# Low halves of gelu moved to VectorE, and the steps around them reordered, in a two-layer graph network kernel

## The chip, the cores and the metric

One core of one Trainium2 chip runs the whole program. The metric is the device time of one launch in microseconds. The engines are TensorE (PE in the rows; PEld is its weight load), VectorE (DVE), ScalarE (ACT), GpSimd (POOL) and SyncE (SP, which issues the DMAs). Each takes its own instructions in the order written and waits on semaphores.

## The reference

```python
# 8 graphs, 1024 nodes, 256 features
h = maximum(layernorm(x), 0)                 # "new-graph norm"
for l in range(3):                           # layers 0 to 2
    si = h @ attn_w[l, :d]; sj = h @ attn_w[l, d:]
    s = leaky(si[:, :, None] + sj[:, None, :] + attn_b[l], 0.2)
    s = where(adj + eye > 0, s, -inf)
    h = layernorm(h + softmax(s) @ h, g1, beta1)
    h = layernorm(h + gelu(h @ W1 + b1) @ W2 + b2, g2, beta2)
x = x + h
h = maximum(layernorm(x), 0)                 # "graph norm" of the last layer
Wh = h @ W                                   # attention products
e = where(adj == 0, -1e9, leaky(Wh @ a1 [:, None] + Wh @ a2 [None, :], 0.2))
x = x + elu(softmax(e) @ Wh)
```

A row of the last layer without any edge gets the plain mean of Wh, for which the kernel needs the sum of Wh over all nodes of a graph.

## The kernel before, in words

The work is 32 steps, `ORDER`, k = 0 to 31; each is one layer of one graph. 24 are feed-forward steps (layers 0 to 2) and 8 are last-layer steps (6, 10, 14, 18, 22, 29, 30, 31). The order on each engine is written out by hand: each engine's block walks the steps with its own `ffn_step` or `gat_step`, and tables such as `MAX_FE`, `UNITS_FE`, `SHIFT_FE` say at which place t (0 to 7, the tiles of the aggregation) or 8 + n (n = 0 to 15, the feed-forward blocks) a piece of the next step's preparation is done. `prep_tables(k)` picks the tables by the kind of step k + 1.

A feed-forward step. TensorE aggregates tile t (`aggregate`, 16 products of pw and xx), VectorE adds the residual and takes its statistics (`residual1`), GpSimd makes the reciprocal deviation (`ln_rstd`), ScalarE normalises (`normalise_pair`), TensorE transposes (`transpose_h`). Then, for block n, `hidden(k, n)` writes one of two PSUM banks FB[n % 2], ScalarE applies gelu and makes the fp16 high half (`gelu`), and the low half, gelu minus its high half, is made by VectorE for even n and by GpSimd for odd n (`g_low` on each). `second(k, n)` multiplies both halves by W2. TensorE's order in block n is: preparation, graph attention pieces, `hidden(k, n + 2)`, `second(k, n)`. Blocks 0 and 1 of hidden stand inside the aggregation of tile 7. For even n + 2, `hidden` waits for VectorE's low half of block n, as it is made from the bank itself. For odd n + 2 it waits only for gelu, since odd gelus are written to a buffer g32 in SBUF, which GpSimd reads.

Preparation of the next step: VectorE's row maxima (`row_max`, tiles 0 to 7, with `shift_columns` after tiles 3 and 7), ScalarE's mask shifts (`shifted_mask`, tiles 0 to 7, at the places of a SHIFT table), then 16 units (`unit` on TensorE, `score` on VectorE, one place later) and `exps` on ScalarE. `scores(q, t)` on VectorE are the two dot products of a tile for step q.

Some steps carry more. RAW_AT: the first norm of a new graph (`raw_statistics`, `ln_rstd(LNR, ...)`, `normalise_pair(LNR, ...)`, `edges`, `self_edges`). GAT_AT: the graph norm and products of a last layer. There ScalarE copies a transposed pair (`gat_pair`), VectorE makes its low half (`gat_low`, tile mj), TensorE multiplies (`gat_product`, bank TH) and ScalarE writes the values (`gat_values`); `gat_colsum` sums them over nodes on TensorE as 8 fp32 products with ones in bank TP, and `gat_sum` copies the sum to csum on VectorE. g = 0 is carried by k=5 in its own order (GAT_FFN_LATE), g = 1 to 6 by k=8, 12, 16, 20, 24, 28, and g = 7 by the last-layer step k=29.

Of the kernel before, what the change touches and what calls it, by code (L numbers as in the profile page):

```python
# [86 lines left out]
GAT_FFN_LATE = {5}  # L87

# [36 lines left out]
SHIFT_FE = {7: (0,), 8: (1,), 9: (2,), 10: (3,), 12: (4, 5), 13: (6, 7)}  # L125
# [3 lines left out]
SHIFT_FC = {7: (0,), 8: (1,), 9: (2,), 10: (3,), 11: (4,), 12: (5,), 13: (6,), 14: (7,)}  # L129
# [4 lines left out]
def prep_tables(k):  # L134
# [9 lines left out]
    if q == 8:  # L144
        return dict(col=None, ct=1, s1=3, sj=5, r2=4, row=MAX_F8, units=UNITS_FE, shift=SHIFT_FE)
# [52 lines left out]
def build(nc, x, adj, attn_w, attn_b, W1, b1, W2, b2, g1, beta1, g2, beta2, gatW, gata, out):  # L198
# [10 lines left out]
    with ctx:  # L209
# [18 lines left out]
        g32 = sb("g32", [P, HALF])  # L228
# [64 lines left out]
        def xgT_of(g):  # L293
            return xgT7 if g == 7 else xgT
# [58 lines left out]
        cs_done = sem("cs_done")  # L353
        wct_done = sem("wct_done")
# [243 lines left out]
        def _(pool):  # L598
# [62 lines left out]
            def g_low(k, n):  # L661
                i = NF * fi(k) + n
                pool.wait_ge(ghi_done, i + 1)
                pool.tensor_tensor(out=gT[:, i % GRING, 1, :], in0=g32[:, :], in1=gT[:, i % GRING, 0, :],  # L664
                                   op=ALU.subtract).then_inc(glo_odd, 1)

# [21 lines left out]
            def ffn_step(k):  # L688
# [17 lines left out]
                else:  # L706
# [8 lines left out]
                    g_low(k, 1)  # L715
                    ln_rstd(LN1, i, 3)
                early = k + 1 not in VERY_LATE
                for n in range(NF):
                    if n % 2 == 1 and not (n == 1 and low_first):
                        g_low(k, n)  # L720
                    if n == 11:
                        ln_rstd(LN2, i, 0)
                    if n in (1, 3, 9, 11):
                        j = (1, 3, 9, 11).index(n)
                        affine(LN1, k, 2 * j)
                        affine(LN1, k, 2 * j + 1)
# [8 lines left out]
                    if raw is not None and early:  # L735
                        if n in (1, 3, 5, 7):
                            ln_rstd(LNR, raw, n // 2)
# [78 lines left out]
        def _(act):  # L816
# [30 lines left out]
            def gelu(k, n):  # L847
# [1072 lines left out]
```

## Time and profile before

| | us |
|---|---|
| median of 3 runs | 2521.38 |
| lowest and highest | 2520.96, 2524.68 |
| the profiled execution | 2526.61 |
| its span, first to last instruction | 2524.9 |
| busy: PE, DVE, ACT, POOL | 2296.6, 1834.2, 1581.8, 1278.9 |
| longest feed-forward steps: k=0, k=24, k=28 | 108.5, 100.7, 99.3 |

The busy times of the engines overlap. A wait row names the engine that stood idle, what it then did, and whose work ended last before it. Times inside the trace are counted from the span's start; step k=9 starts at 820.9 us, k=11 at 939.4, k=12 at 1028.8 and k=26 at 2120.7.

### The profile page before, as it was taken

To read this page: it belongs to the slowest core of one execution; us is meant where nothing else is said; L and a number is where in the kernel's file an instruction comes from. 1 tells how busy PE (TensorE), PEld (TensorE's weight loads), DVE (VectorE), ACT (ScalarE), POOL (GpSimd) and SP (SyncE) were. 2 spreads that over 40 slices of the span, in tenths; PEclk is the share of its full clock that TensorE was granted. 3 is DMA by queue.
4 is the path that set the end of the run, shared out by engine and by line. 5 is a ranking of instruction groups with operands and counts; after the bars stand their busy time and mean duration, and the time that the engine had idled before them with its cause. 6 is when DMAs were issued, how large, how long until landed. Compare 5 with 4: busy or idle time off the path is not lost.

```text
span 2524.9 us, 41684 instructions
## 1 busy us (share of the span) xinstructions
PE 2296.6 (91%) x14721; PEld 1736.3 (69%) x14721; DVE 1834.2 (73%) x4915; ACT 1581.8 (63%) x2426; POOL 1278.9 (51%) x2199
## 2 busy tenths in 40 slices
PE   5899999998899989999998999899998999999977
PEld 4566767766676766767766767677676677676766
DVE  8676678558677786776876878768777676766775
ACT  5467565757566675675766566765756656766654
POOL 4455456653365444663465552745535455545611
PEclk9999999998999999999999999999999999999998
DMA  6312021102210122110211101201131010101000
GB/s 217 109 43 88 9 81 50 57 4 67 76 59 5 38 72 71 59 39 6 92 55 55 43 25 68 87 24 43 40 103 60 1 43 10 38 5 26 22 22 26
DMA packets 66222, 128.57 MB, mean 51 GB/s; under 512 B 12985, under 2 KB 53213, under 8 KB 62942
## 3 DMA queue, kind: packets, MB, share of 16 engines
q1 hardware_dynamic: 66014, 125.90, 14.9%
q8 instruction: 117, 1.92, 0.3%
q14 instruction: 91, 0.75, 0.1%
HBM read 111.20 MB, written 14.68 MB: 50 GB/s over the span
## 4 chain that ended last, share of the span: by engine, by line
PE 52%; DVE 22%; POOL 9%; ACT 8%; issue 8%; DMA 1%; DVEq 0%; SPq 0%; POOLq 0%; ACTq 0%
PE OB L1609 35%; PE FBB L1609 10%; DVE mj L1216 4%; DVE pw L1240 4%; PE RB L1609 3%; DVE junk L1158 2%; ACT nms L888 2%; POOL xc L651 2%; POOL gT L664 2%; PE TH L1609 2%; DVE st L1107 2%; ACT gT L865 2%; POOL rs L633 1%; POOL xc L653 1%; DVE gT L1254 1%
## 5 line engine op out<-in xcount | busy, mean ns | idle before, releaser
L1609 PE MATMUL OB<-xx,pw 128*128 128x257 f32 x4096 | 958.3, 389 | 25.3 <-DVE xc L1134 11.3
L1609 PEld LDWEIGHTS OB<-xx,pw 128*128 128x128 f32 x4096 | 773.5, 193 | 160.4 <-DVE xc L1134 17.4
L1609 PE MATMUL FBB<-hT,wb 128*128 128x512 f16 x2304 | 564.2, 383 | 48.6 <-DVE gT L1254 37.9
L1609 PE MATMUL OB<-wb,gT 128*128 128x256 f16 x4608 | 575.1, 276 | 22.1 <-POOL gT L664 22.1
L1609 PEld LDWEIGHTS OB<-wb,gT 128*128 128x128 f16 x4608 | 453.3, 99 | 159.3 <-POOL gT L664 32.0
L664 POOL TENSOR_TENSOR gT<-g,gT 128x512 f16<-128x512 f32 x192 | 228.3, 1189 | 534.6 <-ACT gT L865 533.5
L1609 PEld LDWEIGHTS FBB<-hT,wb 128*128 128x128 f16 x2304 | 214.6, 98 | 255.0 <-DVE gT L1254 40.7
L871 ACT ACTIVATE pw<-pw,sj 128x512 f32<-128x512 f32 x512 | 336.6, 712 | 65.3 <-DVE pw L1240 64.3
L829 ACT ACTIVATE xc<-xc,nb,rs 128x256 f32<-128x256 f32 x384 | 212.8, 590 | 165.0 <-POOL nb L636 165.0
L651 POOL TENSOR_TENSOR xc<-xc,gb 128x256 f32<-128x256 f32 x384 | 294.0, 766 | 11.4 <-ACT xc L829 11.4
L888 ACT ACTIVATE nms<-nm,cc 128x1024 bf16<-128x1024 bf16 x256 | 281.3, 1136 | 18.7 <-DVE cc L1231 18.7
L1240 DVE SCALAR_TENSOR_TENSOR pw<-r2s,sj,RB 128x512 f32<-128x512 f32 x377 | 268.8, 739 | 32.3 <-PE RB L1609 31.9
L1254 DVE TENSOR_TENSOR gT<-FBB,gT 128x512 f16<-128x512 f32 x192 | 132.0, 687 | 219.8 <-ACT gT L865 218.6
L1216 DVE CUSTOM_DVE_ANT_0 mj<-RB,nm 128x1024 bf16<-128x1024 f32 x224 | 266.1, 1215 | 12.6 <-PE RB L1609 12.6
L628 POOL TENSOR_SCALAR ve<-mv 128x2 f32<-128x2 f32 x256 | 59.2, 231 | 399.9 <-DVE mv L1110 386.8
L860 ACT ACTIVATE FBB<-FBB,wc 128x512 f32<-128x512 f32 x192 | 126.3, 658 | 162.8 <-PE FBB L1609 162.1
L633 POOL TENSOR_TENSOR rs<-ve,mhalf 128x2 f32<-128x2 f32 x256 | 182.9, 715 | 21.3
L860 ACT ACTIVATE g<-FBB,wc 128x512 f32<-128x512 f32 x192 | 130.5, 680 | 100.5 <-PE FBB L1609 100.0
L1609 PE MATMUL RB<-identb,nms 128*128 128x128 bf16 x1508 | 137.4, 225 | 45.4 <-DVE pw L1240 35.9
L1117 DVE RECIPROCAL rden<-OB 128x1 f32<-128x1 f32 x192 | 31.9, 166 | 198.8 <-PE OB L1609 198.4
L1163 DVE CUSTOM_DVE_ANT_0 junk<-xx,aw 128x256 bf16<-128x256 f32 x256 | 163.2, 637 | 0.0
L1107 DVE BATCH_NORM_STATS2 st<-xc 128x6 f32<-128x256 f32 x392 | 156.7, 421 | 6.8
(127 smaller groups left out, 2721.8 us busy)
## 6 DMA issues: line engine op xcount, KB each, us to landing
wb<-w_scratch SPq DMA_DIRECT2D x19, 2048.0 KB, 7.9
adjst<-in_adj SPq DMA_DIRECT2D x56, 512.0 KB, 4.2
xx<-in_x SPq DMA_DIRECT2D x16, 512.0 KB, 5.5
nm<-in_L_gnn_W SPq DMA_DIRECT2D x6, 1024.0 KB, 8.4
gb<-in_L_gnn_g SPq DMA_DIRECT2D x48, 128.0 KB, 2.8
adjst<-in_x SPq DMA_DIRECT2D x6, 1024.0 KB, 10.9
out_x<-adjst SPq DMA_DIRECT2D x48, 128.0 KB, 1.7
pw<-in_adj SPq DMA_DIRECT2D x4, 1024.0 KB, 10.3
```

What stands on the lines that cost most here:

```text
L633: pool.tensor_tensor(out=rs[:, kind, c], in0=ve[:, kind, c], in1=mhalf[:, :], op=ALU.pow)\
L651: pool.tensor_tensor(out=v, in0=v, in1=gb[:, 0, :], op=ALU.mult).then_inc(mul_done[kind], 1)
L664: pool.tensor_tensor(out=gT[:, i % GRING, 1, :], in0=g32[:, :], in1=gT[:, i % GRING, 0, :], op=ALU.subtract).then_inc(glo_odd, 1)
L829: act.activation(dst, src, ACT.Relu if kind in (LNR, LNG) else ACT.Identity, bias=nb[:, kind, t:t + 1], scale=rs[:, kind, t:t + 1])\
L860: act.activation(dst, src, ACT.Gelu, bias=b1c[:, layer(k), f:f + 1], scale=1.0 / W_SCALE)\
L871: act.activation(v, v, ACT.Exp, bias=sj2[:, q % 2, jt:jt + 1]).then_inc(exp_done, 1)
L888: act.activation(nms[:, it, :], nm[:, slot(q), it, :], ACT.Identity, bias=cc[:, it:it + 1])\
L1107: dve.bn_stats(st[:, kind, t % 2, :], src[:, t, 0:D]).then_inc(bs_done[kind], 1)
L1163: dve.tensor_tensor_reduce(out=junk[:, 1, :], in0=src, in1=aw[:, l, 1, :], scale=1.0, scalar=0.0, op0=ALU.mult, op1=ALU.add, accum_out=sc[ ...
L1216: dve.tensor_tensor_reduce(out=mj[:, n % 2, :], in0=row_bank(q)[:, :], in1=nm[:, g % 3, t, :], scale=1.0, scalar=-3e38, op0=ALU.add, op1=A ...
L1240: dve.scalar_tensor_tensor(out=pw[:, jt, half], in0=r2s[:, half], scalar=sj8[:, q % 2, jt:jt + 1], in1=b, op0=ALU.max, op1=ALU.add).then_i ...
L1609: return pe.matmul(o, lhsT, rhs, start=first, stop=last)
```

## The change

- The low half of odd blocks is made by VectorE from the PSUM bank, like the even ones. The buffer g32 and GpSimd's `g_low` go. `hidden(k, n + 2)` now waits for the low half of block n for every n.
- New-graph norms: ScalarE's `normalise_pair(LNR)` moves from n = 2, 4, 6, 8 to n = 5, 7, 8, 9; GpSimd's `ln_rstd(LNR)` goes ahead of the affines of its block.
- `gat_product` stands one block later (n = 6, 8, 10, 12), `gat_values` too (7, 9, 11, 13), and the transposed pairs alternate between two buffers.
- Node sums of graphs 0 to 6: GpSimd adds the eight tiles (`node_sum`, 7 additions), TensorE does one product with ones, mostly in the step after.
- Mask shifts: SHIFT_FE and SHIFT_FC have tiles 0 to 3 at t = 6 and 7, ahead of the first gelu, and tiles 4 to 7 one a block; k=7 keeps the old table as SHIFT_F8.
- Scores of tiles 0 to 3 for steps 11, 15, 19, 23 move from the step three before them to n = 1, 3, 5, 7 of the step two before. `ln_rstd(LN2, i, 1)` and the second LN2 pair come one block earlier.

```diff
+SUM_AT = {k if k in GAT_FFN_LATE else k + 1: g for k, g in GAT_AT.items() if g < 7}
-SHIFT_FE = {7: (0,), 8: (1,), 9: (2,), 10: (3,), 12: (4, 5), 13: (6, 7)}
+SHIFT_FE = {6: (0, 1), 7: (2, 3), 11: (4,), 12: (5,), 13: (6,), 14: (7,)}
+SHIFT_F8 = {7: (0,), 8: (1,), 9: (2,), 10: (3,), 12: (4, 5), 13: (6, 7)}
-SHIFT_FC = {7: (0,), 8: (1,), 9: (2,), 10: (3,), 11: (4,), 12: (5,), 13: (6,), 14: (7,)}
+SHIFT_FC = {6: (0, 1), 7: (2, 3), 10: (4,), 11: (5,), 12: (6,), 13: (7,)}
...
+        xgT_odd = sb("xgT_odd", [P, 2, KD, 2 * P], f16)
...
-            return xgT7 if g == 7 else xgT
+            return xgT7 if g == 7 else xgT_odd if j % 2 else xgT
...
@@ gpsimd ffn_step
-                    if n % 2 == 1 and not (n == 1 and low_first):
-                        g_low(k, n)
+                    if raw is not None and early and n in (1, 3, 5, 7):
+                        ln_rstd(LNR, raw, n // 2)
+                    if n == (9 if k in GAT_FFN_LATE else 5) and k in SUM_AT:
+                        node_sum(SUM_AT[k])
...
+                if gat == 6:
+                    node_sum(gat)
...
+            def node_sum(g):
+                acc = csum[:, g % 2, :]
+                v = xx[:, g % 3, :, 0:D]
+                for t in range(1, NT):
...
+                    pool.tensor_tensor(out=acc, in0=v[:, 0, :] if t == 1 else acc, in1=v[:, t, :],
+                                       op=ALU.add).then_inc(part_done, 1)
@@ scalar
-                if n % 2 == 1:
-                    if i >= 2:
-                        act.wait_ge(glo_odd, i // 2)
-                    dst = g32[:, :]
-                else:
-                    dst = src
...
-                    if raw is not None and early and n in (2, 4, 6, 8):
-                        normalise_pair(LNR, raw, n // 2 - 1)
+                    if raw is not None and early and n in (5, 7, 8, 9):
+                        normalise_pair(LNR, raw, (5, 7, 8, 9).index(n))
-                        if n in (6, 8, 10, 12):
-                            gat_values(gat, n // 2 - 3)
+                        if n in (7, 9, 11, 13):
+                            gat_values(gat, (n - 7) // 2)
-                    if n == 15:
+                    if n == 14:
                         normalise_pair(LN2, k, 1)
@@ vector ffn_step
-                    if n % 2 == 0 and n > 0:
+                    if n > 0:
                         g_low(k, n)
+                    if n == 14 and k in SUM_AT and k not in GAT_FFN_LATE:
+                        gat_sum(SUM_AT[k])
+                    if k + 2 in AHEAD and n in (1, 3, 5, 7):
+                        scores(k + 2, n // 2)
@@ tensor
                 if i >= 2:
-                    if i % 2 == 0:
-                        pe.wait_ge(glo_even, i // 2)
-                    else:
-                        pe.wait_ge(gelu_done, i - 1)
+                    pe.wait_ge(glo_odd if i % 2 else glo_even, i // 2)
...
-                    if early and n in (5, 7, 9, 11):
-                        gat_product(gat, (n - 5) // 2)
+                    if early and n in (6, 8, 10, 12):
+                        gat_product(gat, (n - 6) // 2)
...
-                    if gat is not None and n == 14:
-                        gat_colsum(gat)
+                    if k in SUM_AT and n == (14 if k in GAT_FFN_LATE else 13):
+                        gat_colsum(SUM_AT[k])
```

## Rows read from the trace of the kernel before

**Rows 1.** the page's part 1: busy us, share of the span, instructions

```profile
PE 2296.6 (91%) x14721; PEld 1736.3 (69%) x14721; DVE 1834.2 (73%) x4915; ACT 1581.8 (63%) x2426; POOL 1278.9 (51%) x2199
```

**Rows 2.** by stretch (k=11, 12, 9): PE, PEld, DVE, ACT, POOL busy, clock, DMA

```profile
939.40:1028.80 89.40, 79.94 (x533) 59.37 (x530) 66.81 (x169) 54.09 (x83) 47.63 (x81) 0.99 0.21 68
1028.80:1124.40 95.60, 89.56 (x595) 68.08 (x594) 70.16 (x184) 60.95 (x97) 54.38 (x97) 0.99 0.13 40
820.90:904.90 84.00, 79.56 (x531) 59.05 (x531) 59.83 (x163) 51.26 (x78) 42.55 (x72) 1.00 0.10 34
```

**Rows 3.** waits of PE: us in total, times, longest us

```profile
PE FBB L1609 <- DVE gT L1254: 37.9, 32, 3.1
...
PE OB L1609 <- POOL gT L664: 22.1, 23, 2.6
PE TH L1609 <- DVE mj L1291: 19.1, 13, 2.6
```

**Rows 4.** groups by form: shapes, count, busy us, mean ns, idle before

```profile
L1240 DVE SCALAR_TENSOR_TENSOR pw<-r2s,sj,RB 128x512 f32<-128x512 f32 x377 | 268.8, 739 | 32.3 <-PE RB L1609 31.9
L1216 DVE CUSTOM_DVE_ANT_0 mj<-RB,nm 128x1024 bf16<-128x1024 f32 x224 | 266.1, 1215 | 12.6 <-PE RB L1609 12.6
L664 POOL TENSOR_TENSOR gT<-g,gT 128x512 f16<-128x512 f32 x192 | 228.3, 1189 | 534.6 <-ACT gT L865 533.5
...
L1163 DVE CUSTOM_DVE_ANT_0 junk<-xx,aw 128x256 bf16<-128x256 f32 x256 | 163.2, 637 | 0.0
...
L1254 DVE TENSOR_TENSOR gT<-FBB,gT 128x512 f16<-128x512 f32 x192 | 132.0, 687 | 219.8 <-ACT gT L865 218.6
...
L1609 PE MATMUL TP<-xx,onesf 128*128 128x256 f32 x128 | 29.3, 381 | 0.0
```

**Rows 5.** timeline of k=12, first blocks: start us, duration us, instruction, [idle before]

```profile
1056.95 1.13 ACT L888 ACTIVATE nms<-nm,cc 128x1024 bf16<-128x1024 bf16 x1
...
1058.10 1.28 ACT L860 ACT_TABLE_LOAD   x1
...
1059.86 0.66 ACT L860 ACTIVATE FBB<-FBB,wc 128x512 f32<-128x512 f32 x1 [0.48 <-PE FBB L1609]
...
1061.19 0.69 DVE L1254 TENSOR_TENSOR gT<-FBB,gT 128x512 f16<-128x512 f32 x1 [0.38 <-ACT gT L865]
...
1063.13 1.46 PE L1609 MATMUL FBB<-hT,wb 128*128 128x512 f16 x6
...
1069.94 1.47 PE L1609 MATMUL FBB<-hT,wb 128*128 128x512 f16 x6 [1.00 <-DVE gT L1254]
```

**Rows 6.** timeline of k=12, later blocks

```profile
1082.78 1.48 PE L1609 MATMUL TH<-gw,mj 128*128 128x256 f16 x12 [1.29 <-DVE mj L1291]
...
1100.20 0.94 DVE L1163 CUSTOM_DVE_ANT_0 junk<-xx,aw 128x256 bf16<-128x256 f32 x1
...
1103.57 0.42 DVE L1163 CUSTOM_DVE_ANT_0 junk<-xx,aw 128x256 bf16<-128x256 f32 x1
...
1117.73 3.67 PE L1609 MATMUL TP<-xx,onesf 128*128 128x256 f32 x16
```

**Rows 7.** timeline of k=11, two waits

```profile
986.58 1.47 PE L1609 MATMUL FBB<-hT,wb 128*128 128x512 f16 x6 [2.02 <-ACT g L860]
...
1026.58 2.42 PE L1609 MATMUL OB<-wb,gT 128*128 128x256 f16 x12 [2.55 <-POOL gT L664]
```

**Rows 8.** the table by stretch, just after the second of them

```profile
1026.50:1029.00 2.50, 2.42 (x13) 1.90 (x14) 0.76 (x2) 2.50 (x5) 2.34 (x5) 0.59 0.00 0
```

**Rows 9.** timeline of k=9: low half 0, and the start of k=10

```profile
853.45 0.69 DVE L1254 TENSOR_TENSOR gT<-FBB,gT 128x512 f16<-128x512 f32 x1
...
904.89 7.21 PE L1609 MATMUL OB<-xx,pw 128*128 128x257 f32 x32 [1.22 <-DVE xc L1134]
```

**Rows 10.** timeline of k=26, blocks 1 to 3

```profile
2158.03 1.46 PE L1609 MATMUL FBB<-hT,wb 128*128 128x512 f16 x6
...
2160.27 0.68 DVE L1248 TENSOR_TENSOR hT<-TH,hT 128x512 f16<-128x512 f32 x1
```

More of the change, by code:

```diff
@@ L144, in prep_tables @@
     if q == 8:
-        return dict(col=None, ct=1, s1=3, sj=5, r2=4, row=MAX_F8, units=UNITS_FE, shift=SHIFT_FE)
+        return dict(col=None, ct=1, s1=3, sj=5, r2=4, row=MAX_F8, units=UNITS_FE, shift=SHIFT_F8)
     if q == 7:
@@ L353, in build @@
         cs_done = sem("cs_done")
+        part_done = sem("part_done")
         wct_done = sem("wct_done")
@@ L659, in self_edges @@
                 pool.tensor_tensor(out=d, in0=d, in1=notib[:, :], op=ALU.mult).then_inc(dfix_done, 1)
[L661 to L665, printed above, removed]
             def x1_add(g, t):
@@ L714, in ffn_step @@
                         ln_rstd(LNG, gat, 1)
-                    g_low(k, 1)
                     ln_rstd(LN1, i, 3)
@@ L782, in gat_step @@
                     final(g, t)
+            def node_sum(g):
+                acc = csum[:, g % 2, :]
+                v = xx[:, g % 3, :, 0:D]
+                for t in range(1, NT):
+                    if t == 1 or t % 2 == 0:
+                        pool.wait_ge(wv_done, 4 * g + t // 2 + 1)
+                    if t > 1:
+                        pool.wait_ge(part_done, 7 * g + t - 1)
+                    pool.tensor_tensor(out=acc, in0=v[:, 0, :] if t == 1 else acc, in1=v[:, t, :],
+                                       op=ALU.add).then_inc(part_done, 1)
             def biases():
@@ L1289, in gat_low @@
                 dve.wait_ge(pth_done, 4 * g + j + 1)
-                v = xgT_of(g)
+                v = xgT_of(g, j)
                 dve.tensor_tensor(out=v[:, 1, :, :], in0=TP[:, :, :], in1=v[:, 0, :, :],
@@ L1489, in ffn_step @@
                             scores(GAT_STEP[gat], n - 8)
-                    if nxt is not None and n >= 14 and k + 2 not in AHEAD and k not in GAT_FFN_LATE:
+                    if k + 2 in AHEAD and n in (1, 3, 5, 7):
+                        scores(k + 2, n // 2)
+                    if nxt is not None and n >= 14 and k + 2 not in AHEAD and k + 3 not in AHEAD \
+                            and k not in GAT_FFN_LATE:
                         scores(nxt, n - 14)
@@ L1499, in ffn_step @@
                 statistics2(k, 3)
-                if gat is not None:
+                if k in GAT_FFN_LATE:
                     gat_sum(gat)
@@ L1505, in ffn_step @@
                     mask_rows(k + 2, MAX_AHEAD[END])
-                elif nxt is not None:
+                elif nxt is not None and k + 3 not in AHEAD:
                     if k in GAT_FFN_LATE:
@@ L1535, in gat_step @@
                         score(k + 1, u)
+                    if k == 29 and t == 3:
+                        gat_sum(6)
                     if k == 30 and t == 6:
@@ L1793, in gat_colsum @@
             def gat_colsum(g):
-                pe.wait_ge(wv_done, 4 * g + 4)
+                if g < 7:
+                    pe.wait_ge(part_done, 7 * g + 7)
+                else:
+                    pe.wait_ge(wv_done, 4 * g + 4)
                 pe.wait_ge(*tp_after[-1])
-                for jt in range(NT):
-                    ins = mm(TPf[:, 0:D], onesf[:, :], xx[:, g % 3, jt, 0:D], jt == 0, jt == NT - 1)
+                if g < 7:
+                    ins = mm(TPf[:, 0:D], onesf[:, :], csum[:, g % 2, :], True, True)
+                else:
+                    for jt in range(NT):
+                        ins = mm(TPf[:, 0:D], onesf[:, :], xx[:, g % 3, jt, 0:D], jt == 0, jt == NT - 1)
                 ins.then_inc(cs_done, 1)
@@ L1870, in gat_step @@
                             gat_transpose(gat, t - 4)
+                    if k == 29 and t == 2:
+                        gat_colsum(6)
                     if k == 30 and t == 5:
```

20 lines of the change are left out of this document (9 added, 11 removed).

## The prediction, made before the changed kernel was run

> **What bounds the kernel now.** I read the page's busy shares first: TensorE is busy 2296.6 of 2524.9 us [rows 1]. It works through one order written out by hand, so every wait of TensorE is time, and a wait of another engine is time only where TensorE then waits for it. Second came the table by stretch. Of the 32 steps, 24 are feed-forward steps (aggregation of 8 tiles, then 16 blocks n = 0 to 15). I took one of each kind that repeats: k=11 carries a new graph's norms, k=12 the graph attention products, k=9 only its own work [rows 2]; k=26 is like k=9 with later tables. TensorE is idle 9.5, 6.0 and 4.4 us in the three, by subtraction. VectorE is busy 66.8 and 70.2 us of 89.4 and 95.6 in the first two: the second most loaded engine, and it gets more work. Third, TensorE's waits by releaser: 37.9 us for the low halves that VectorE makes (next hidden product into the same bank), 22.1 us for those of GpSimd, and 19.1 us for the attention low halves [rows 3]. Those are what the change goes for. Last I walked the timelines, for the order in which each engine meets its work.
>
> **The direct terms.** *Node sums.* Eight fp32 products with ones, 16 instructions a graph, take 3.67 us each time [rows 6], 29.3 us for all eight graphs [rows 4]. For graphs 0 to 6 one product of the eight stays: 7 x 3.67 x 7/8 = 22.5 us of TensorE work goes. GpSimd gets 7 x 7 = 49 additions of half the width of a low half (1189 ns [rows 4]), so 29 to 58 us and about 37 by my estimate, in places where it has been waiting 533.5 us for ScalarE's copies [rows 4]; I cost them at nothing. At the end of k=28 they stand ahead of the next norm's statistics, which VectorE delivers about as late. If that cover were gone, up to 5 us would show once.
>
> *Odd low halves.* 192 operations of 1189 ns leave GpSimd, and 192 of 687 ns come to VectorE [rows 4]: +132 us there, 8 x 0.69 = 5.5 us in each of 24 steps. Two things change for TensorE. The product of block n waits 0.5 us less for its low half. But the hidden product n+2, which for odd n waited only for gelu (it went to a buffer in SBUF), now waits for VectorE's low half of n, behind whatever is queued there, and that is one product (1.3 us) earlier in TensorE's order.
>
> *Shifts.* The tables move four mask shifts of ScalarE ahead of the first gelu, where one stood (the other three lay behind gelu 0, gelu 1 and the norm pair 3). This holds for 14 steps: ten with SHIFT_FE (4, 8, 11, 12, 15, 16, 19, 20, 24, 28), four with SHIFT_FC (9, 13, 17, 21).
>
> **Walk through k=12** (times from its rows). ScalarE ends norm pair 2 at about 1057.0, then come one shift of 1.13 us, the table load of 1.28, and 0.48 us of waiting before gelu 0 at 1059.86; the low half ends at 1061.88, and hidden 2 starts at 1063.13 [rows 5]. With four shifts: 1057.0 + 4 x 1.13 + 1.28 = 1062.8 for gelu 0, 1064.1 with its copy, 1064.8 with the low half. Hidden 2 starts 1.7 us late. VectorE holds tile 7's residual behind that low half (about 1.3 us), then a row maximum (1.2 [rows 4]) and the statistics of graph attention (about 0.95), and only then the new low half of n = 1 (0.7): 1068.9. TensorE wants it at 1064.8 + 2.8 = 1067.6, another 1.3 us lost. The old 1.00 us wait of hidden 4 [rows 5] goes into that. At the end of block 2 I am 2.4 to 2.8 us behind.
>
> From block 3 on it comes back. GpSimd no longer stands at low half 3, so the second graph norm comes by my estimate 1.8 us earlier, and gelu 5 with it. The product moved a block later doesn't meet its 1.29 us wait [rows 6], but the next transposition needs the same attention low half, which now stands behind low half 5 (about 1084.5), so about 1.8 us is waited for there. Equal by block 7. In blocks 8 to 15 VectorE carries a low half in each block plus a unit score, 0.74 [rows 4], and a pair of attention scores, 0.9 to 1.8: 2.3 to 3.2 us, 4.3 where the residual or a norm's statistics join, against some 2.8 us of TensorE and 4.2 where a product stands. It is just about full. The column sum's 3.67 us leaves the step, and the last low half then holds TensorE for about 1 us. Taken over the step: -3.7 us for the sum, +1.7 for VectorE's queue, so -2 us at the next aggregation. Bounds: -5 (nothing new waited for) to +1 (every score at the slow figure). Six steps (8, 12, 16, 20, 24, 28): **-12 us**.
>
> **k=11.** The odd gelu 3 waited behind a new-graph norm: hidden 5 lost 2.02 us, and the last product 2.55 us for GpSimd [rows 7]. After the 2.55 us the granted clock was 0.59 in the next 2.5 us [rows 8], near the lower of the two levels (1.2 GHz against 2.4), and those 12 instructions took 2.42 us [rows 7]. The norms move to n = 5 to 9, which takes some 5 us of waits and 1 of clock away. The shifts and low half 1 give 1.5 back, and VectorE's second half (a low half, a score pair and a unit in every block) another 2: -3 for 11, 15, 19 and -2.5 for 7 (bounds -6 and +1). **-11.5 us**.
>
> **k=9 and its three likes** have few waits to lose. Low half 0 ended at 854.1 [rows 9], held by row maxima; with four shifts it would be 856.5, and low half 1 again comes about 1.2 us after it is wanted: +3. Nothing later absorbs it, as TensorE has no other long wait there. The remaining product of the column sum is 0.46. At the end VectorE is late already: TensorE waits 1.22 us for the residual [rows 9], and low half 15 and the copy of the sum (0.69 + 0.40) stand before it in its queue. +4.2 each, 4 steps: **+17 us** (bounds +1 and +6 each). The scores moved into n = 1 to 7 lie in idle time of VectorE and cost nothing; the one at n = 1 is counted in the lateness.
>
> **k=26 and its likes** (1, 2, 25, 26, 27): low half 1 comes after row maxima 2 and 3 and the shift columns, whose end is at 2160.3, where ht's low half starts; hidden 3 started at 2158.03 [rows 10]. It would start at 2161.0, 2.9 us late. The wait of hidden 4, like the 1.00 us of k=12, goes, and some of the rest: +1.5 at block 2, +0.3 at the end, and a wait as long as the 2.55 us above may lower the clock again, up to 1 us: +2.5 each, **+12.5 us** (bounds +0.7 and +4). k=4 has the shifts and no wait to win: **+2.5**. k=0, 3 and 23 have VectorE late through most of their blocks, so the 5.5 us show in part: +3 each, **+9**. k=5 saves its sum but pays its low halves, -1.5; one product more in k=29, +0.5: **-1**.
>
> **Sum:** -12 - 11.5 + 17 + 12.5 + 2.5 + 9 - 1 = **+16.5 us**. The profiled run took 2526.6 us with a span of 2524.9, so it becomes 2543; it stands 5.2 above the median of the runs, 2521.4, so the forecast is **2538 us**.
>
> **A rule beside a row.** The score of one tile took 0.94 us at 1100.20 and 0.42 at 1103.57 [rows 6]; its mean is 637 ns [rows 4], so 256 of them lose 256 x 0.22 = 56 us. GpSimd was inside a tensor operation at 1100.20 and idle at 1103.57. With GpSimd's work down from 1278.9 by 228 - 37 = 191 us, 15%, some 8 us of the 56 would go, and about as much for the other scores. I count it within the bounds.
> The Trainium skill (SBUF — State Buffer, section SBUF: two separate sides) says that a VectorE operation with two SBUF inputs and a GpSimd operation that reads SBUF take one port pair exclusively, the later one blocking in full. By that rule VectorE is freed exactly where the scores fill it, and the node sums block it again where they run; that is the mechanism of the first rival.
>
> **Rivals.**
> 1. *VectorE keeps up (faster).* Place: blocks 8 to 15 of the heavy steps. If the score pairs run at 0.9 us because GpSimd has nothing left but affines that it can do early, k=12's kind gains 5 (not 2), k=11's kind 5 (not 3), and the light steps find their row maxima and small operations done sooner, so that low half 1 loses 1 us less in 20 steps: -18 - 8 - 20 = -46 against my sum, less 16 for places where GpSimd's affines now meet the row work: -30, so 2538 - 30 = **2508 us**. It decides once the second halves run without TensorE waiting. For it: 219.8 us in which VectorE stood before a low half, waiting for ScalarE's copy [rows 4]. Against: that idle time is mostly in blocks 3 to 7, not where the queue is long.
> 2. *It cancels.* The shifts find more slack than 0.48 us, or the late low half 1 costs half: -15, **2522 us**.
> 3. *VectorE saturates (slower still).* If each of 13 heavy steps (the kinds of 11 and 12, and 0, 3, 23) loses 1.5 us more through scores at 1.8 us a pair, and clock drops follow: +20, **2557 us**.
> 4. *The change doesn't do what it says*: the double buffer leaves the wait where it is, since the transposition needs the same low half. That is in the sum already.
>
> **How the numbers follow.** Forecast 0.45, rival 1 0.29, rival 2 0.16, rival 3 0.10. About 0.2%, 5 us, is what a measurement tells from no change. Slower: forecast and rival 3, 0.55. Faster: mostly rival 1, 0.30. Within: 0.15. The range 2500 to 2562 takes in three rivals and leaves the far ends of the bounds out. The forecast's own range is 2527 to 2552.
>
> **What would show it.** Per step: gelu 0 about 2.9 us later in 14 steps, and hidden 2 waiting 1 to 2 us for low half 0; hidden 3 waiting for low half 1 in the light steps, 2.9 us in k=26; TensorE's waits for VectorE's gelu low halves up from 37.9 to about 100 us, for GpSimd's gone; k=9's length 84.0 to about 88, k=12's 95.6 to about 93.6, k=11's 89.4 to 86.4. Wrong if k=9 stays near 84 or k=12 drops below 91: then VectorE's queue is shorter at the low halves than I walked it.

## The result, and the profile after

The changed kernel takes **2492.0 us** (median of 4 runs, 2487.8 to 2492.9) against 2523.0 for the kernel before (4 runs, 2521.0 to 2525.2): ratio 0.987, 95% interval 0.986 to 0.989. It is 1.3% faster, where I forecast 0.7% slower with a range that ended at 2500 us. The profiled execution took 2492.9 us with a span of 2491.2, 33.7 us less than before. Two kernels further down had one execution each far above the others (2562.5 us for e10_fills_no_wait, 8173.9 us for b4_sum6_early), which their medians and ratios leave out. The page's part 1, answering [rows 1]:

```profile
PE 2262.1 (91%) x14623; PEld 1715.4 (69%) x14623; DVE 1902.4 (76%) x5107; ACT 1576.9 (63%) x2426; POOL 1089.6 (44%) x2056
```

The same stretches as in [rows 2], k=11, 12 and 9, and k=26 as a fourth (us from the span's start; length; PE, PEld, DVE, ACT, POOL busy; granted clock; DMA share, GB/s):

```profile
935.60:1017.70 82.10, 78.47 (x534) 58.94 (x531) 70.36 (x178) 52.62 (x81) 38.15 (x73) 1.00 0.23 75
1017.70:1108.00 90.30, 84.99 (x577) 64.50 (x577) 67.72 (x184) 59.24 (x94) 44.48 (x88) 1.00 0.13 42
814.00:900.90 86.90, 79.97 (x532) 59.16 (x532) 67.20 (x179) 54.64 (x84) 38.79 (x71) 1.00 0.10 34
2086.90:2169.20 82.30, 78.74 (x513) 58.47 (x513) 58.19 (x155) 52.54 (x80) 34.09 (x64) 0.98 0.03 7
```

k=11 went from 89.4 to 82.1 us, k=12 from 95.6 to 90.3, k=9 from 84.0 to 86.9, k=26 from 79.9 to 82.3. Over the whole span, by the kinds of the prediction (differences of the steps' lengths in the two traces):

| steps | forecast, us | measured, us |
|---|---|---|
| k=12 kind (8, 12, 16, 20, 24, 28) | -12 | -31.3 |
| k=11 kind (11, 15, 19) and 7 | -11.5 | -25.6 |
| k=9 kind (9, 13, 17, 21) | +17 | +11.6 |
| late (1, 2, 25, 26, 27) | +12.5 | +8.6 |
| k=4 | +2.5 | -0.8 |
| 0, 3, 23 | +9 | -2.0 |
| 5, 29 | -1 | +7.0 |
| the rest, with what stands ahead of k=0 | 0 | -1.2 |
| sum | +16.5 | -33.7 |

So both losing kinds lost, somewhat less than forecast, and the heavy steps gained twice to three times as much as I gave them. The rows with k=0 and k=29 are less sure than the others: in the traces of kernels that change nothing in these two steps, k=0 takes 106.3 to 109.0 us and k=29 48.3 to 51.6. TensorE's waits (us in total, times, longest), answering [rows 3]:

```profile
PE FBB L1621 <- DVE gT L1259: 85.6, 68, 3.1
...
PE OB L1621 <- DVE xc L1139: 15.5, 21, 1.9
...
PE OB L1621 <- DVE gT L1259: 7.5, 10, 1.8
...
PE TP L1783 <- DVE csum L1301: 4.3, 1, 4.3
...
PE TH L1621 <- DVE mj L1296: 2.2, 1, 2.2
PE TP L1783 <- DVE mj L1296: 2.1, 6, 0.3
```

Waits for GpSimd's low halves are gone (22.1 us), those of the next hidden product for VectorE's rose from 37.9 to 85.6, and the wait of the attention product fell from 19.1 to 2.2 us without coming back at the transposition (2.1). VectorE's groups, answering [rows 4] (shapes, count, busy us, mean ns, idle before):

```profile
L1259 DVE TENSOR_TENSOR gT<-FBB,gT 128x512 f16<-128x512 f32 x384 | 262.6, 684 | 211.7 <-ACT gT L870 211.3
...
L1168 DVE CUSTOM_DVE_ANT_0 junk<-xx,aw 128x256 bf16<-128x256 f32 x256 | 152.0, 594 | 0.0
...
L1163 DVE CUSTOM_DVE_ANT_0 junk<-xx,aw 128x256 bf16<-128x256 f32 x256 | 122.3, 478 | 0.3 <-issue 0.3
```

The 192 new low halves cost VectorE 131 us, but it is only 68 us busier: the row products of a tile (two SBUF operands) fell from 637 and 570 ns to 594 and 478 ns, 35 us together. The other 28 us are spread over smaller groups and overlaps, which I did not trace.

The two mechanisms of loss stand where the walk put them. k=12, first blocks (start, duration, instruction, [idle before]), answering [rows 5]:

```profile
1045.17 4.25 ACT L893 ACTIVATE nms<-nm,cc 128x1024 bf16<-128x1024 bf16 x4
1049.44 1.28 ACT L865 ACT_TABLE_LOAD   x1
1050.74 0.66 ACT L865 ACTIVATE FBB<-FBB,wc 128x512 f32<-128x512 f32 x1
...
1052.81 1.47 PE L1621 MATMUL FBB<-hT,wb 128*128 128x512 f16 x6 [1.28 <-DVE gT L1259]
...
1056.71 1.47 PE L1621 MATMUL FBB<-hT,wb 128*128 128x512 f16 x6 [1.12 <-DVE gT L1259]
...
1060.56 1.47 PE L1621 MATMUL FBB<-hT,wb 128*128 128x512 f16 x6 [0.64 <-DVE gT L1259]
```

Four shifts now stand ahead of gelu 0. Hidden 2 waits 1.28 us for low half 0, and hidden 3 another 1.12 us for low half 1, which stands behind a residual, a row maximum and statistics (1.3 was forecast); the last row is hidden 4, which waits 0.64 us for low half 2, where it waited 1.00. And k=26:

```profile
2126.94 2.74 PE L1621 MATMUL FBB<-hT,wb 128*128 128x512 f16 x6 [2.80 <-DVE gT L1259]
```

2.80 us, where I had written 2.9. The 2.74 us for work that takes 1.47 is the clock at the lower of its two levels behind the wait: the granted clock was 0.50 from 2126.9 to 2129.7 us.

### The profile page after: what moved, and what is told of

Its sections match the earlier page's. It is cut to its first block, busy times and chain, and to the rows that moved or that the text cites. A ratio compares the mean times of both kernels' runs of the same rounds, so it can differ in the third digit from the quotient of the medians.

```text
span 2491.2 us, 41367 instructions
## 1 busy us (share of the span) xinstructions
PE 2262.1 (91%) x14623; PEld 1715.4 (69%) x14623; DVE 1902.4 (76%) x5107; ACT 1576.9 (63%) x2426; POOL 1089.6 (44%) x2056
## 4 chain that ended last, share of the span: by engine, by line
PE 55%; DVE 26%; ACT 7%; issue 6%; POOL 5%; DMA 1%; SPq 0%; DVEq 0%; POOLq 0%; ACTq 0%
PE OB L1621 35%; PE FBB L1621 12%; DVE pw L1245 5%; DVE mj L1221 4%; PE RB L1621 3%; DVE gT L1259 3%; ACT nms L893 3%; DVE st L1112 2%; PE TH L1621 2%; DVE junk L1163 2%; POOL rs L636 1%; DVE xc L1139 1%; DVE xc L1126 1%; ACT FBB L865 1%; ACT L865 1%
## 5 line engine op out<-in xcount | busy, mean ns | idle before, releaser
L1621 PE MATMUL FBB<-hT,wb 128*128 128x512 f16 x2304 | 563.7, 383 | 86.0 <-DVE gT L1259 85.6
L865 ACT ACTIVATE FBB<-FBB,wc 128x512 f32<-128x512 f32 x384 | 253.0, 659 | 284.0 <-PE FBB L1621 282.9
L1259 DVE TENSOR_TENSOR gT<-FBB,gT 128x512 f16<-128x512 f32 x384 | 262.6, 684 | 211.7 <-ACT gT L870 211.3
L654 POOL TENSOR_TENSOR xc<-xc,gb 128x256 f32<-128x256 f32 x384 | 292.5, 762 | 33.4 <-ACT xc L840 33.3
L870 ACT ACTIVATE gT<-FBB 128x512 f16<-128x512 f32 x384 | 229.3, 597 | 12.1
L636 POOL TENSOR_TENSOR rs<-ve,mhalf 128x2 f32<-128x2 f32 x256 | 184.6, 721 | 21.3
L656 POOL TENSOR_TENSOR xx<-xc,gb 128x256 f32<-128x256 f32 x192 | 147.4, 768 | 15.1
L656 POOL TENSOR_TENSOR xc<-xc,gb 128x256 f32<-128x256 f32 x192 | 146.0, 760 | 15.1
```

Of the source, the lines that this page charges most:

```text
L636: pool.tensor_tensor(out=rs[:, kind, c], in0=ve[:, kind, c], in1=mhalf[:, :], op=ALU.pow)\
L654: pool.tensor_tensor(out=v, in0=v, in1=gb[:, 0, :], op=ALU.mult).then_inc(mul_done[kind], 1)
L656: pool.tensor_tensor(out=o, in0=v, in1=gb[:, 1, :], op=ALU.add).then_inc(aff_done[kind], 1)
L865: act.activation(src, src, ACT.Gelu, bias=b1c[:, layer(k), f:f + 1], scale=1.0 / W_SCALE)\
L870: act.activation(gT[:, i % GRING, 0, :], src, ACT.Copy).then_inc(ghi_done, 1)
L1259: dve.tensor_tensor(out=gT[:, i % GRING, 1, :], in0=FB[i % 2][:, :], in1=gT[:, i % GRING, 0, :], op=ALU.subtract).then_inc(glo_odd if n % ...
```

## Experiments: the edits one by one

Every run is compared with the kernel before on the same chip; a gain or loss against the changed kernel (2492.0 us, ratio 0.987) is the difference of two such ratios times 2524 us. The intervals are about 0.0015 of the ratio each side, so single differences are good to some 5 us; lengths of a repeated step, from the traces, are sharper.

**Low halves alone** (e2_low_only), the kernel before with

```diff
-    if n % 2 == 0 and n > 0:
+    if n > 0:
         g_low(k, n)          # VectorE; GpSimd's g_low, g32 and its waits left out
```

> The kernel before, only the odd gelu low halves moved from GpSimd to VectorE. Theory A (the low halves are where my heavy steps were mis-sized): 22.1 us of waits for GpSimd and most of 16 us behind its norm queue go, 48 us of waits for VectorE come less what it had, VectorE's row work gets 35 us shorter: 2522 - 15 = 2507 us. Rival (as I forecast, with the gain in the other edits): +10 to +20, 2532 to 2542 us.

2510.5 us, ratio 0.995 (0.993 to 0.996): 13 us faster than before, nearly theory A. Moving work onto the second most loaded engine was a gain by itself. By steps, against the kernel before: the k=11 kind (with 7) falls by 18.0 us (k=11 to 85.0), the k=12 kind by 8.0 (k=12 to 94.6), k=0, 3 and 23 by 5.8; k=9 and its likes are 1.4 us longer each, the five late steps 10.0 in all. In k=9 the loss is hidden 3, which did not wait before:

```profile
852.01 1.47 PE L1593 MATMUL FBB<-hT,wb 128*128 128x512 f16 x6 [1.32 <-DVE gT L1238]
```

**Shifts back** (e1_shifts_back), the changed kernel with the tables SHIFT_FE and SHIFT_FC of before.

> The changed kernel with the two shift tables as before. My walk: four shifts ahead of gelu 0 start it 2.9 us later in 14 steps and cost TensorE about 2 us in each, so 2492 - 28 = 2464 us, k=9 back from 86.9 to about 84.5 us. Rival: the shifts were in the way of gelus 0 to 2 and of the norm pair where they stood, so putting them back delays gelu 2 and hidden 4: no gain, 2490 to 2505 us.

2469.7 us, ratio 0.978 (0.977 to 0.980): 22 us better than the changed kernel. The mechanism is shown, but not 2 us a step: the 14 steps with the moved shifts are 0.5 to 1.8 us shorter, 1.4 on average and 19.2 in all. k=9 is 85.1, k=12 88.8, and TensorE's waits for VectorE's low halves fall from 85.6 to 69.4 us. Hidden 3 of k=9 still waits 1.32 us for low half 1. The two stretches:

```profile
808.20:893.30 85.10, 79.79 (x532) 59.21 (x532) 66.90 (x179) 54.52 (x84) 38.65 (x71) 1.00 0.10 35
1009.60:1098.40 88.80, 84.82 (x577) 64.55 (x577) 67.84 (x184) 59.32 (x95) 44.41 (x88) 1.00 0.13 43
```

**Attention scores back** (e4_scores_back)

```diff
-    if k + 2 in AHEAD and n in (1, 3, 5, 7):
-        scores(k + 2, n // 2)
-    if nxt is not None and n >= 14 and k + 2 not in AHEAD and k + 3 not in AHEAD ...
+    if nxt is not None and n >= 14 and k + 2 not in AHEAD ...
-    elif nxt is not None and k + 3 not in AHEAD:
+    elif nxt is not None:
```

> The changed kernel with the attention scores of the steps after next as before: of k=11, 15, 19, 23 back at the end of k=8 kind (two in blocks 14 and 15, two behind the last statistics) in place of blocks 1 to 7 of k=9 kind. Theory A, I missed a gain at the end of k=8, 12, 16, 20, where VectorE is late: +3.5 us each, k=12 from 90.3 to about 94, 2492 + 14 = 2506 us. Rival, as forecast: they cost nothing at either place, 2490 to 2495 us.

2495.5 us, ratio 0.988 (0.986 to 0.990): the time alone can't tell the two. The steps can: k=8, 12, 16 and 20 are each 1.6 to 1.8 us longer (k=12 is 92.1), k=9 and its likes 0.2 to 0.4 shorter, together 5.6 us longer. Theory A in kind, at half its size.

**Products and one buffer back** (e7_products_back)

```diff
-    if early and n in (6, 8, 10, 12):
-        gat_product(gat, (n - 6) // 2)
+    if early and n in (5, 7, 9, 11):
+        gat_product(gat, (n - 5) // 2)   # gat_values a block earlier too, xgT alone
```

> The changed kernel with the attention products in blocks 5, 7, 9, 11 again and their one buffer. Theory A, a block of delay removes the wait for the attention low half for good: the 17 us of TensorE's waits for it come back, and VectorE's queue is longer than before: 2492 + 18 = 2510 us. Rival, my fourth one: the transposition waits for the same low half, so nothing was won: 2490 to 2495 us.

2500.4 us, ratio 0.991 (0.989 to 0.993): 9 us slower, half of theory A; by steps, 1.8 to 3.6 us in each of the six. TensorE's wait for the attention low half is back in part:

```profile
PE TH L1621 <- DVE mj L1296: 11.6, 19, 2.2
```

My fourth rival, which I had put into the sum, is wrong: the wait did not move to the transposition.

**New-graph norms back** (e6_norms_back)

```diff
-    if raw is not None and early and n in (5, 7, 8, 9):
+    if raw is not None and early and n in (2, 4, 6, 8):    # ScalarE; GpSimd behind its affines
```

> The changed kernel with the new-graph norms back in blocks 2, 4, 6, 8 of ScalarE and behind the affines on GpSimd. Theory A, it is the norm between two gelus that cost k=11 its 2 us waits: +3 us in each of k=3, 7, 11, 15, 19, 2492 + 15 = 2507 us. Rival: the waits came from GpSimd, whose queue no longer holds low halves: 2490 to 2496 us.

2498.7 us, ratio 0.990 (0.989 to 0.992): 8 us slower; k=11, 15 and 19 are 3.7 to 4.0 us longer each and k=3 and 7 are not. Theory A in three of its five steps, and a half of k=11's gain of 7.3 us.

**Node sums back on TensorE** (e5_sums_back): gat_colsum again with eight products, node_sum left out, its place (block 13 of the step after) kept.

> The changed kernel, the node sums again as eight fp32 products with ones on TensorE, GpSimd's additions left out. By my term: 7 x 3.67 x 7/8 = +22.5 us, 2514.5 us. Rival: at n = 13 VectorE is late anyway, so a part of the 3.2 us is hidden behind the wait for its low half: +10 to +15 us, 2502 to 2507 us.

2500.9 us, ratio 0.991 (0.989 to 0.993): +9.6 us, the rival's figure but not its reason. k=9 and its likes and k=25 are 2.8 to 3.0 us longer, 14.3 in all, so of the 3.2 us a step that I had priced almost all shows and little is hidden. What brings the total down lies in other steps (k=0, 2, 5 and 29 are 1.4 to 2.6 us shorter in this trace), of which k=0, 2 and 29 differ by as much between traces without any edit there. k=12 doesn't change, since its 3.67 us left with the move of the sum to the next step, which this run keeps.

## Experiments: GpSimd's work, and where VectorE is full

**Spare operations on GpSimd** (e3_spare_ops), at the places of its old low halves:

```diff
+    pool.wait_ge(ghi_done, i + 1)
+    for c in range(2):        # ... each waits for the one before it
+        pool.tensor_tensor(out=spare, in0=aw[:, 0, c, :], in1=gw[:, 0, c, :], op=ALU.subtract)
```

> The changed kernel, and at the places where GpSimd made an odd low half it now does two subtractions of 128x256 from constants into a tile that nobody reads (1.4 us in place of 1.19). The output is the same. Theory A, GpSimd's work with SBUF operands slows VectorE's: the products of L1163 go back from 594 to about 640 ns, VectorE busy +35 us or more, TensorE loses about half of it: 2492 + 18 = 2510 us. Rival B: only GpSimd's own queue mattered: VectorE's durations stay, 2492 to 2497 us.

2550.5 us, ratio 1.010 (1.008 to 1.012): **+58 us** for work that nobody waits for, three times theory A. So I took the wait and the operations apart, and then the operands.

**The wait alone** (e8_wait_only): the first line of that diff, without the loop.

> The changed kernel, and at the places where GpSimd made an odd low half it now only waits for ScalarE's copy of that block, with no operation. In the run with two subtractions there (2550.5 us) the chain was: norm pair 3's statistics behind the wait, gelu 3 behind the norm pair, low half 3 behind gelu 3. Theory A, the wait in GpSimd's queue is what costs: at least 35 of the 58 us return, 2527 us or more. Rival B, the operations' own time and their use of SBUF are what costs: 2492 to 2500 us.

2513.3 us, ratio 0.995 (0.993 to 0.996): +19 us. The steps show a loss and a gain in it: the six steps of the k=12 kind are 21.3 us longer, k=0 and k=5 6.2 and 4.3 us shorter. I did not follow up why the wait helps those two.

**The operations without the wait** (e9_ops_no_wait).

> The changed kernel with the two subtractions of GpSimd at each such place, but they wait for nothing. Theory A (the wait): GpSimd does them early, while it would be idle, TensorE loses only what VectorE's longer products give, 2492 to 2502 us. Rival B (the operations): most of the 58 us stays, 2530 us or more. By either, the products of VectorE with two SBUF inputs lengthen where they meet the subtractions, from 594 ns to above 620.

2526.8 us, ratio 1.001 (1.000 to 1.002): +34 us. Neither half explains the 58 alone; together they make 53, which is 58 within the intervals. The theories of both runs, which looked for one cause, were too simple.

**Fills in place of the subtractions** (e10_fills_no_wait): six pool.memset of a 128x256 tile at each place, no wait.

> The changed kernel, and at each place where GpSimd made an odd low half it fills a tile with zeros six times, waiting for nothing (no operand is read from SBUF; I expect about 1.2 us in all, as the two subtractions took 1.4). The subtractions there cost 34.5 us (2526.8). Theory P (operands in SBUF): VectorE's second product goes back to about 594 ns and TensorE loses under 10 us: 2492 to 2502 us. Theory Q (GpSimd's time in its queue, ahead of the norms): the same loss as with the subtractions, times 1.2 / 1.4: about 2520 us.

2519.7 us (median of 9), ratio 0.999 (0.998 to 1.000): +29 us. The fills took 1.9 us a place, not 1.2. Run with subtractions first, with fills second:

```profile
L671 POOL TENSOR_TENSOR spare<-aw,gw 128x256 f16<-128x256 f32 x384 | 272.5, 710 | 16.7
...
L1181 DVE CUSTOM_DVE_ANT_0 junk<-xx,aw 128x256 bf16<-128x256 f32 x256 | 166.8, 652 | 0.0
```
```profile
L671 POOL MEMSET spare<- 128x256 f16 x1152 | 360.5, 313 | 56.2
...
L1180 DVE CUSTOM_DVE_ANT_0 junk<-xx,aw 128x256 bf16<-128x256 f32 x256 | 147.8, 577 | 0.0
```

Reading SBUF lengthens VectorE's second product (652 ns here and 643 with the waits, against 594 in the changed kernel and 569 to 611 in the other variants of the changed kernel); writing alone doesn't (577). But the first product stays at 484 ns. The move of the low halves alone had taken the two from 570 and 637 ns to 482 and 547, so reads at the same places bring back the second and not the first; why the first fell is open. VectorE is 39 us busier with the subtractions and 12 with the fills. But 29 us are lost with the fills too. So most of it goes with GpSimd's time in its own queue (theory Q), by whatever that delays; per us of GpSimd's work the fills cost 0.08 us and the subtractions 0.125, and only that surplus, some 12 of the 34 us by my estimate, is left for the operands.

What the queue does shows in the wait-only run's k=12. There GpSimd held its two affines back until ScalarE's copy of block 3 was done, which is just when VectorE begins its eight corrections of the edges (three SBUF operands). The wait-only run, then the changed kernel:

```profile
1060.56 0.72 POOL L654 TENSOR_TENSOR xc<-xc,gb 128x256 f32<-128x256 f32 x1 [2.43 <-ACT gT L876]
...
1061.35 3.77 DVE L1296 SCALAR_TENSOR_TENSOR nm<-ident,dgm,nm 128x128 bf16<-128x128 f32 x8
```
```profile
1063.74 0.72 POOL L656 TENSOR_TENSOR xc<-xc,gb 128x256 f32<-128x256 f32 x1
...
1064.69 2.19 DVE L1290 SCALAR_TENSOR_TENSOR nm<-ident,dgm,nm 128x128 bf16<-128x128 f32 x8
```

In the changed kernel the last affine ends at 1064.46, 0.2 us before the corrections. With the wait they meet, and the eight take 3.77 us in place of 2.19; in the fills run, where two affines come late behind the fills, 3.18, so a part of what fills cost is this meeting too; in the spare-operations run, beside a spare subtraction and four affines, 4.69. There TensorE waits 3.87 us for the unit score behind them and then runs for a while at the lower clock (granted 0.61 from 1083.1 to 1085.8; the next 6 hidden products take 2.41 us, not 1.47):

```profile
1083.12 0.40 PE L1635 MATMUL RB<-identb,nms 128*128 128x128 bf16 x4 [3.87 <-DVE pw L1259]
1083.35 2.41 PE L1635 MATMUL FBB<-hT,wb 128*128 128x512 f16 x6
```

The Trainium skill (SBUF — State Buffer, section SBUF: two separate sides) says that a VectorE operation with two SBUF inputs and a GpSimd operation that reads SBUF hold one port pair exclusively. The traces agree in that such operations of VectorE take longer beside GpSimd's reads and not beside its fills: 2.19 against 4.69 us for the same eight operations, and 652 against 577 ns beside reads and beside fills. That the pair is held for a whole instruction no run here shows; beside the 2.19 us four small operations of GpSimd on 128x2 tiles run, the longest 0.70 us, without lengthening them visibly.

**Is the meeting the cause?** (e13_wait_edges_later, and its control e14_edges_later): the corrections moved from block 3 to block 4, with the wait and without it.

```diff
-    if n == 3:
+    if n == 4:
         gat_edges(gat)
```

> The kernel in which GpSimd only waits at the old places of its low halves (2513.3 us), with VectorE's eight edge corrections of a new graph (128x128, three operands in SBUF) in block 4 in place of block 3 of the six steps that carry attention norms. In that run they took 3.77 us in k=12 beside two affines of GpSimd, against 2.19 us in the changed kernel, and then TensorE waited 3.0 us for a unit score. Theory: the meeting is the cause, and in block 4 GpSimd is done: their mean back from 504 to about 370 ns, k=12 from 94.5 to about 91, six such steps: 2513.3 - 20 = 2493 us. Rival: the delay of the norm behind GpSimd's wait is what costs: they get shorter, but the time stays at 2508 to 2513 us.

> The control: the changed kernel with the same move of the edge corrections to block 4. There they meet nothing at block 3 as it is (368 ns), so: 2490 to 2494 us. If block 4 is a better or worse place by itself, this run shows by how much, and the other is to be read against it.

The control is the surprise: 2508.2 us, ratio 0.994 (0.993 to 0.996), 18 us slower. In block 4 the corrections delay the first attention low half, and a transposition of TensorE waits 2.5 us for it in each of six steps:

```profile
PE TP L1783 <- DVE mj L1296: 15.3, 6, 2.5
```

With the wait: 2516.3 us, ratio 0.998 (0.997 to 0.999), and the corrections take 360 ns each, as unhindered (504 in the wait-only run). So my forecast for the first run was wrong (2493), but against its control the wait now costs 9 us (0.998 against 0.994), where it cost 19 with the corrections in its way; in the six steps alone 6.6 us, where it was 21.3. That is consistent with the meeting as half of the wait's price or more, but not proof of the share: the control has a wait of its own in the same steps, which can hide a delay of the norms behind it.

**Where VectorE is full** (e11_vec_late_blocks and e12_vec_early_blocks): two subtractions of VectorE ahead of its low half in blocks 9 to 15, or in blocks 1 to 3.

```diff
+    if k in range(7, 29) and n >= 9:        # the other run: 1 <= n <= 3
+        spare_pair()
     if n > 0:
         g_low(k, n)
```

> The changed kernel with two more subtractions of VectorE (128x256, some 0.7 us together) ahead of its low half in each of blocks 9 to 15 of the 18 feed-forward steps from k=7 to k=28: 126 places, 88 us of VectorE's time. My forecast held VectorE to be just about full in blocks 8 to 15: then half or more is waited for, +44 us or more, 2536 us or more. Rival: it had room there, which is the step that I got wrong: under +15 us, 2492 to 2507 us.

> The same two subtractions ahead of the low halves of blocks 1, 2 and 3 in the same steps: 54 places, 38 us of VectorE's time. TensorE waits for low halves 1 and 2 there, so by my walk the 0.7 us of blocks 1 and 2 each show in full: at least +25 us, 2517 us. Rival: blocks 1 to 3 take it up as the others do: under +8 us, 2500 us.

Late blocks: 2574.0 us, ratio 1.020 (1.018 to 1.022), +82 us for 131 us of work (each took 520 ns, not 350). k=11 grows by 6.7 us for the 7.3 added, k=12 by 4.9, k=9 by 3.6, k=26 by 1.9. Early blocks: 2520.1 us, ratio 0.999 (0.998 to 1.000), +29 us for 67 us of work, 2.4 in k=9, 2.4 in k=26, only 0.7 in k=12. So my premise, VectorE just about full in blocks 8 to 15, is right for the k=11 kind; k=12 took up a third of the added work there, and the light steps about half or more. The waits of TensorE in k=11, changed kernel first, then with the late spare work:

```profile
PE FBB L1621 <- DVE gT L1259: 1.5, 2, 1.3
PE TP L1621 <- DVE cT L1196: 1.2, 1, 1.2
PE OB L1621 <- DVE xc L1139: 0.5, 1, 0.5
PE OB L1621 <- DVE gT L1259: 0.4, 1, 0.4
```
```profile
PE FBB L1635 <- DVE gT L1261: 5.2, 5, 1.8
PE OB L1635 <- DVE gT L1261: 2.8, 2, 1.9
```

In k=11 the changed kernel stands just on the near side of the brink.

## Experiments: better versions

**Low half 1 early** (b1_low1_early)

```diff
+    # at t == 7, behind residual1(k, 7)
+    g_low(k, 1)
...
-    if n > 0:
+    if n > 1:
         g_low(k, n)
```

> The changed kernel with VectorE's low half 1 straight behind the residual of tile 7, ahead of the row maxima and statistics of block 0. By my walk low half 1 comes 1.1 to 2.8 us late in every feed-forward step; without that: -1.2 us in 19 steps and -2.8 in k=25, 26, 27, 1, 2: 2492 - 37 = about 2460 us if nothing else is late, 2470 as my middle value. Rival: the row maxima become late in its place, and hidden 4 waits instead: 2488 to 2495 us.

2484.4 us, ratio 0.985 (0.983 to 0.986): -7 us, a fifth of what the waits promised. The late steps give 8.8 us, but in k=9 and 12 nothing is won (+0.3 and 0.0): hidden 3 no longer waits and hidden 4 does, 1.23 and 1.94 us, as the rival said. k=7 loses 2.6.

**With the shifts back** (b2_low1_shifts), and with low half 1 early only in k=1, 2, 25, 26, 27 (b3_late_low1_shifts).

> The changed kernel with both: shifts as before and low half 1 early. Theory A: the two gains lie in different steps (late steps and the 14 steps with the moved shifts): 2469.7 - 8 = 2462 us. Rival: with gelu 0 back in time, low half 1 is again the last to come in k=9 and k=12 (1.3 and 2.1 us of TensorE's waits there), so it wins there too: 2445 us.

> The changed kernel with the shifts as before and low half 1 early in k=1, 2, 25, 26, 27 alone. Theory: those five steps give 8.8 us, k=0 and 7 lose nothing as they did with all steps early (1.4 and 2.6 us): 2469.7 - 9 = 2461 us. Rival: by the clock's chance, nothing: 2468 us.

2466.0 (ratio 0.976, 0.975 to 0.978) and **2462.9 us (0.976, 0.974 to 0.977)**: the gains add up, not the rival's. The second is 2.4% faster than the kernel before and beats both kernels; against the first its lead is within the intervals.

**Node sum of graph 6 copied earlier in k=29** (b4_sum6_early), on top of that: gat_sum(6) ahead of tile 3's work.

> The changed kernel with shifts as before, low half 1 early in k=1, 2, 25, 26, 27, and in k=29 the copy of the node sum ahead of the row maxima of tile 3, as a transposition of TensorE waits 4.3 us for it. Theory: k=29 falls from 51.6 to about 48 us, 2462.9 - 3.5 = 2459.5 us. Rival: the attention norm there is late too, or the row maxima become the last: 2462 to 2464 us.

2463.4 us (median of 3), ratio 0.976 (0.974 to 0.978): no gain, and k=29 stays at 51.7 us. The 4.3 us wait is gone. In its place one product waits 3.7 us for the attention norm and a transposition 1.5 us for ScalarE; the 2.7 us of a later product stay. Without and with this edit, and the kernel before all of this:

```profile
PE TP L1786 <- DVE csum L1302: 4.3, 1, 4.3
...
PE TH L1624 <- DVE wb L1297: 2.7, 1, 2.7
```
```profile
PE TH L1624 <- DVE wb L1297: 6.3, 2, 3.7
```
```profile
PE TH L1609 <- DVE wb L1291: 6.0, 2, 3.4
```

The attention norm was the real limit; the copy had only stood in front of it.

## Why the prediction was wrong, by its own steps

**The step that failed** is the price of the moved low halves on VectorE: 2 us a step in k=11's second half, 1.7 in k=12's, 3 in each of k=0, 3 and 23, while what the shorter queue of GpSimd gives back was counted too low. The run with only the low halves moved shows 13 us less, where that part of my account had 10 to 20 more; k=11 is 4.4 us shorter by it, k=12 0.9, and k=0, 3 and 23 5.8 together. A second step failed beside it: terms of other edits that I had put at nothing (the later product, the scores that leave k=12's kind) are worth 9 and 2 to 6 us.

**k=12, "-3.7 for the sum, +1.7 for VectorE's queue, so -2"**: the sum is -5.3, and -6.3 in k=28. The -3.7 is there (TensorE's busy time falls by 4.6, from 89.56 to 84.99). The shifts cost 1.5 us over the step, where I had walked 2.4 to 2.8 us behind at block 2 and nothing left by block 7, so that is a loss I had missed. The low halves alone gave 0.9, where I had charged 1.7 for the queue. And two terms I had set to nothing were gains. *The product moved a block later*: I said its wait would be met at the transposition (about 1.8 us in place of the 1.29). It was not: six such waits sum to 2.1 us over the kernel, and putting it back costs 1.8 to 3.6 us a step. Whether that is the second buffer or ScalarE's copies of the values a block later I didn't take apart. *The moved scores*: I priced them only where they arrive (nothing, nearly right: 0.4 us in k=9) and forgot that they leave the end of k=8, 12, 16 and 20, where VectorE is late: 1.7 us each. One by one these pieces make some -6.6 in k=12, so they overlap by more than a us.

**k=11, "-3"**: -7.3 there, -6.1 and -6.5 in 15 and 19. I took 6 us away and gave 3.5 back. The removal was close: these two waits of TensorE in k=11 of the kernel before are gone, half of them by the norms' move (3.7 to 4.0 us).

```profile
PE OB L1609 <- POOL gT L664: 3.4, 3, 2.5
PE FBB L1609 <- ACT g L860: 3.3, 2, 2.0
```

The give-back was the error: 1.5 for shifts and low half 1 measured 0.5 to 0.8 (shifts back), and 2 for VectorE's second half is 0.7, two waits of 0.29 and 0.37 us. (6 less 3.5 is also 2.5 and not the 3 that I wrote.) "Just about full" was shown true in this kind of step, and it does not mean late. I added a price for each operation as if the queue were past its brink; it had about 0.6 us left over seven blocks (7.3 us added cost 6.7).

**k=0, 3, 23, "+3 each"**: -2.0 in all, 11 us off. I had charged the new low halves there too, and the run with them alone has -2.3, -1.1 and -2.5; k=0's part is no more than its own spread.

**k=9, +4.2**: +2.9, in the right direction. The +3 for its first blocks was right: hidden 2 waits 1.47 us for low half 0, by the shifts, and hidden 3 1.44 for low half 1, which costs 1.3 to 1.4 without the shifts too (low halves alone). The remaining product is 0.46, and the wait for the residual at the end is 1.9 us, 0.7 more than in [rows 9] and not the 1.1 of the two operations ahead of it. (With those 1.1 my own terms add to 4.5, not 4.2.) What I left out are small gains, the last product's 0.47 us wait for GpSimd first of all. **Late steps, +2.5**: +1.7 on average, and +2.0 by the low halves alone; the wait came as walked, 2.80 us, and a low clock behind it in some of them. Moving low half 1 took the loss away. **k=5 and 29, -1**: +7.0. I had counted too little against the saved products. In k=5 (+4.3) VectorE is 6.3 us busier (61.3 to 67.6) and TensorE's idle time rises from 8.4 to 14.2 us. In k=29 (+2.8) a transposition waits 4.3 us for the copy of the sum, but that takes the place of two other waits: TensorE is idle 8.1 us before and 7.9 after. The granted clock fell from 0.96 to 0.90, and by the spread of this step no cost of the edit is shown there.

**Rival 1**, to which I gave 0.29 at 2508 us, had the right sign. Its place is right (TensorE has almost no waits in the second halves of k=11), but its mechanism is a part only: the shorter row products give VectorE 35 us, while the parts above gave TensorE its time by GpSimd's and ScalarE's queues. Its condition, low half 1 a us less late in the light steps, did not come. Saturation (rival 3) needed as little as 1 us more a block to come true. The edits one by one make: low halves -13, sums, norms, products and scores -10, -8, -9 and -2, shifts +23, in all -19 where -31 was measured. Each of the six is good to 4 or 5 us, so the missing 12 may be pairs that help each other or the runs' scatter; I didn't settle it.

## What to carry to other kernels

An engine that is just full costs almost nothing, and one that is past full can cost nearly every us, as in k=11: find the slack per iteration and compare it with what is added, and don't give each added operation a share of its time. Price a moved operation at both ends, where it leaves as well as where it arrives. And a wait that stands out in the list may only stand in front of another that ends at the same time; look at what its waiter would wait for next before you promise the gain.

## What of the hardware was not expected

- **Idle work on GpSimd is not free.** 268 us of operations that nobody waits for, with a wait ahead of each pair, cost TensorE 58 us, and 19 us with the waits alone. They lengthen VectorE's operations with two SBUF operands where they meet (eight corrections from 2.19 to 4.69 us), and they decide what meets what.
- **The same wait does or doesn't cost clock.** In k=2 hidden 3 waits 2.8 us for low half 1 both in the changed kernel and with the shifts back, with TensorE idle 3.2 us in the step in each; one is 82.2 us long, with a part of it at the lower of the two levels (1.2 of 2.4 GHz), the other 80.5 without. In k=31, which no experiment edits, TensorE is idle 8.5 us in every trace; the step takes 42.1 to 42.7 us at a granted clock of 0.86 to 0.91, and in one trace 39.4 at 0.98 (b3_late_low1_shifts and b4_sum6_early):

```profile
2416.80:2458.90 42.10, 33.60 (x162) 28.30 (x160) 16.83 (x50) 17.79 (x31) 5.81 (x8) 0.91 0.08 26
2416.90:2456.30 39.40, 30.88 (x162) 26.38 (x160) 16.84 (x50) 17.69 (x31) 5.79 (x8) 0.98 0.08 27
```

  So a single step of one trace is good to about 3 us, and the account rests on differences that repeat in the steps of a kind.
